# Leaving out the filling multiplications between the first 24 score blocks of an attention kernel

## What is computed

```
q = _fq_sym(q, axis=-1); k = _fq_sym(k, axis=-1); v = _fq_sym(v, axis=2)
attn = jnp.einsum('bhqd,bhkd->bhqk', q, k)
attn = jax.nn.softmax(attn.astype(jnp.float32), axis=-1)
attn = _fq_unsigned(attn, axis=-1)
out = jnp.einsum('bhqk,bhkd->bhqd', attn, v)
```

## Time and profile before

| | |
|---|---|
| three runs | 1157.61, 1159.09, 1159.81 us (median 1159.09) |
| the profiled execution | 1157.37 us |
| span of its instructions | 1155.7 us |
| mean granted TensorE clock | 0.998 |
| preparation up to the first block | 0 to 67.1 us |
| blocks 0 to 23 on TensorE | 67.1 to 80.9 us |
| attention | about 81 to 712 us |

### The profile page before, as it was taken

One profiled execution on the slowest core, in us unless ns is written; L12 is line 12 of the kernel. 1 busy time (PEld: TensorE's weight loads), 2 busy tenths in 40 slices (PEclk: granted clock), 3 DMA queues, 4 the chain that ended last, 5 costly groups with the idle time before them and its releaser, 6 DMA issues.

```text
span 1155.7 us, 24019 instructions
## 1 busy us (share of the span) xinstructions
PE 1042.3 (90%) x8274; PEld 602.8 (52%) x8388; DVE 945.5 (82%) x1732; ACT 892.8 (77%) x1546; POOL 700.7 (61%) x625
## 2 busy tenths in 40 slices
PE   8988888888888888888888888999999999999997
PEld 4744444444444444444444446756654465557775
DVE  6999999999999999999999996963327888943335
ACT  4799999999999999999999997645533576834441
POOL 3027888888787888888788877247751000653432
PEclk9999999999999999999999999999999999999999
DMA  6799998888798788887875775847928002523336
GB/s 195 123 177 139 174 172 161 170 171 172 167 174 169 169 167 175 172 158 164 170 116 110 115 107 92 261 143 213 325 99 329 1 1 52 175 89 106 101 94 235
DMA packets 388799, 176.36 MB, mean 153 GB/s; under 512 B 330413, under 2 KB 373650, under 8 KB 388680
## 3 DMA queue, kind: packets, MB, share of 16 engines
q1 hardware_dynamic: 381976, 157.85, 63.1%
q0 software_dynamic: 6480, 16.77, 4.3%
q10 hardware_dynamic: 224, 0.20, 0.1%
HBM read 52.70 MB, written 43.59 MB: 83 GB/s over the span
## 4 chain that ended last, share of the span: by engine, by line
PE 46%; DVE 27%; ACT 15%; issue 6%; POOL 3%; DMA 2%; SPq 0%; ACTq 0%; POOLq 0%; DVEq 0%
DVE top L425 21%; ACT weight L485 11%; PE bank L234 7%; PE bank L220 7%; PE bank L1206 4%; PE bank L2641 4%; PE bank L1605 3%; PE bank L252 3%; PE bank L2657 3%; PE bank L1193 2%; PE bank L1182 2%; POOL weight L537 1%; PE bank L684 1%; PE bank L1878 1%; PE bank L1623 1%
## 5 line engine op out<-in xcount | busy, mean ns | idle before, releaser
L485 ACT ACTIVATE weight<-bank,bias,sq_all 128x1024 uint8<-128x1024 f32 x512 | 610.1, 1201 | 14.0 <-PE bank L234 8.8
L425 DVE TENSOR_REDUCE top<-bank 128x1 f32<-128x512 f32 (+1 forms) x683 | 610.2, 951 | 11.2 <-PE bank L220 0.9
L537 POOL CAST weight<-turned 128x2048 bf16<-128x2048 uint8 x256 | 479.5, 1895 | 39.0 <-DMA turned<-weight 19.3
L234 PE MATMUL bank<-kT,query 128*128 128x512 bf16 x918 | 284.2, 381 | 26.9 <-ACT weight L485 12.8
L252 PEld LDWEIGHTS bank<-v_sb,weight 128*128 128x128 bf16 x4096 | 172.1, 97 | 104.7 <-POOL weight L537 2.9
L220 PE MATMUL bank<-kT,qspace 64*128 64x512 bf16 x687 | 134.9, 386 | 55.9 <-DVE top L425 55.9
L252 PE MATMUL bank<-v_sb,weight 128*128 128x16 bf16 x4096 | 172.5, 169 | 2.2 <-POOL weight L537 1.8
L220 PE MATMUL bank<-kT,query 128*128 128x512 bf16 x329 | 124.8, 379 | 2.1 <-DVE top L425 1.4
L234 PEld LDWEIGHTS bank<-kT,query 128*128 128x128 bf16 x1024 | 59.7, 96 | 104.2 <-ACT weight L485 62.0
L1848 POOL DMA_INDIRECT dispatched_rows<-qspace,put x32 | 37.2, 1162 | 116.0 <-DVE qspace L2398 106.9
L485 ACT ACTIVATION_READ_ACCUMULATOR weight<-bank,bias,sq_all 128x1 f32 x512 | 101.3, 198 | 0.0
(11 more groups left out here) (351 smaller groups left out, 1459.2 us busy)
## 6 DMA issues: line engine op xcount, KB each, us to landing
dispatched_rows<-zeros SPq DMA_DIRECT2D x32, 524.0 KB, 3.2
answered_rows<-zeros SPq DMA_DIRECT2D x16, 512.0 KB, 3.2
late<-answered_rows SPq DMA_DIRECT2D x16, 512.0 KB, 6.7
erow<-dispatched_rows SPq DMA_DIRECT2D x39, 131.0 KB, 2.1
wgu<-in_L_ffn_w_gate SPq DMA_DIRECT2D x26, 176.0 KB, 3.7
wgu<-in_L_ffn_w_up SPq DMA_DIRECT2D x26, 176.0 KB, 3.6
query<-qspace SPq DMA_DIRECT2D x32, 128.0 KB, 3.2
turned<-weight SPq DMA_TRANSPOSE x256, 3.2
```

The lines of the kernel that those rows point to most:

```text
L234: mm = pe.matmul(unit[u % 2][:, v * 512:(v + 1) * 512], query2[:, t % 2, h, :], kT[:, h // 2, first + v * 512:first + (v + 1) * 512], star ...
L425: ve.tensor_reduce(top[:, first:first + count], bank[:, first % 3:first % 3 + count, :], AX.X, ALU.max).then_inc(s_max, 1)
L485: ac.activation(weight8[:, n % BYTES, u * 1024:(u + 1) * 1024], unit[u], ACT.Exp, bias=bias[:, n:n + 1], scale=sq_all[:, n:n + 1], accum_o ...
L537: po.tensor_copy(weight[:, n % 3, :, :, :].rearrange("p c q two -> p (c q two)"), turned8[:, n % 3, :, :].rearrange("p c q -> p (c q)").bi ...
```

## The change

The two calls of `stir` in the loop over blocks 9 to 23 are left out, on TensorE alone. The waits, blocks and their order stay; so do the passes at the kernel's beginning and the twelve ahead of the first block.

```diff
                     block = fill_maxima(pe, block, 1)
                     while block < LEAD:
-                        stir(2, 4)
                         block = fill_maxima(pe, block, 2)
-                        stir(2, 4)
                         block = fill_maxima(pe, block, 1)
                     copied(("turned values", 3))
```

## The result

The change makes the kernel slower: 1160.87 us against 1158.12 us, medians of 20 runs each, a ratio of 1.0026 (not exactly the quotient of the two medians, 1.0024) with a 95% interval of 1.0014 to 1.0039. That is 2.75 us, a little more than the 0.2%, 2.3 us, that the prediction counted as nothing. One of the 20 runs of the changed kernel took 1172.71 us with a mean clock of 0.949; no trace shows it, and the median doesn't hang on it. The profiled execution took 1161.26 us, with a span of 1159.5 us and a mean granted clock of 0.992 in place of 0.998.

The account below looks back on a forecast made before the run. VectorE's unbroken reductions were taken to bound the loop. Work, gaps, start of the attention and clock each counted 0, so the forecast stayed at the median of before, 1159.1 us, with a range of 1157.6 to 1161.9.

Parts of the forecast that it names:

- the likeliest case: Loop and opening of the attention: TensorE's clock holds, no difference, 1159.1 us; chance 0.47.
- second case: Clock falls in the loop, rises early in the attention: +1.4 us, 1160.5 us; chance 0.38 for 0.2 to 2.8 us.
- The fillings do no work that anyone waits for: Loop, 72.20 to 81.60 us: 4.3 us of TensorE work hidden by VectorE's reductions; removing it gains 0.
- The clock: Loop: TensorE's busy share drops to 44%, yet its clock was taken to hold; cost 0, both ends kept.
- for it: Argument for a clock fall in the loop: 44% is less than any busy stretch in the trace shows.
- What a fall costs: Loop and attention opening: 0.5 us for two cold cycles plus 0.95 us in the opening, together +1.4 us.
- the short fall: Clock low from the loop into the early attention: +1.4 us, ends 0.2 and 2.8 us; chance 0.38.
- a cold cycle: Three blocks of the loop at the low clock: 1.97 us in place of 1.74, 0.23 us more.
- It isn't won back: Attention after a fall: the delay stays, since VectorE and ScalarE each have but 2% free.
- No DMA, no semaphore and no queue is touched: Whole kernel: the change was said to leave transfers, signals and queues alone, so 0 from them.
- four cold cycles and two rises of the clock: Loop and attention opening: upper end of the short fall, 2.8 us, which set the range's top at 1161.9.
- The rival of a long fall: Clock low from 75 to 95 us, up to the first sums of values: +4.1 us, 1163.2 us; chance 0.08.

Follow-up runs that it names:

- e4: Kernel before with all 20 loop fillings thinned to 32 columns in place of 512; +1.47 us against before.
- e6: The change, unchanged, run again beside the kernel before on one chip; median 3.15 us above before.
- e8: The change with nine fillings added in the waits at 733 and 780 us; 1157.90 us, +0.24 us against before (ratio 1.0000).
- e12: The change with 20 multiplications of 32 columns put into TensorE's waits between 8 and 16 us; median 1.63 us above before.
- the clean pair: The change against the kernel before, both with nine fillings at 733 and 780 us; 1157.90 against 1156.73 us.

## Why the prediction was right or wrong

**The number held, the likeliest case didn't.** 1160.87 us lies in the range of 1157.6 to 1161.9, but above the 1159.1 forecast; "slower" by its own measure of 0.2%, which is what came, had a chance of 0.14. What came are the signs of its second case: pairs of 0.61 us, double reductions 1.96 us apart, the first sum of values late. Point by point:

- *The fillings do no work that anyone waits for.* Right. With ten of twenty left VectorE still has no gap.
- *The clock.* This is the step that failed: "Forty-four per cent lies between these two, nearer to the upper row, and no pause comes near to 3 us. I take 0". The row it leaned on was at 62%, and wasn't the sparsest: from 1036.4 to 1039.4 us before was busy for 1.50 of 3.00 us at a clock of 1.00. Neither lasts as long as the loop, and no row showed a clock held at 44%, as the text itself said under "for it", so the trace gave no ground to lean to that side. The run showed a fall after 3.6 us of blocks alone, with no pause over 0.84 us; in the four other profiles with no filling or thin ones in the loop (e4, e6, e8, e12) it came between 74.9 and 76.4 us. The rule of the Trainium skill that was weighed there (TensorE: Matmul & The Clock Gate, A second HAM failure mode: psum-queue depth-cycling) fits this trace better than the forecast did: the clock fell with small pauses only, between groups that cycle through banks, though once in the loop and not again and again.
- *What a fall costs.* Right in sum: +1.4 us was forecast for the short fall, 1.47 us was read at the first sums of values (1.25 to 1.65 us in the other profiles with the same fall) and 1.41 us at the end of the attention; the clean pair gave 1.17 us. The parts: a cold cycle of 1.97 us was forecast and 1.96 measured. More of it lay in the loop than forecast: from the pair at 82.21 against the warm 81.59 three cold cycles make 0.62 us, not two 0.46; the opening then cost 0.85 us. The 0.95 us of the forecast is a slip, for 4.0 / 4.53 x 1.05 is 0.93; the rest of the difference fits a clock that was back at 86.0 us, before the cycle with two units had ended: the two opening cycles lost 0.20 and 0.63 us.
- *It isn't won back.* Right, to a few hundredths, from 97 to 716 us. Both profiles belong to those that lose 0.6 us near 122 us (see the last section), so that doesn't show in their difference.
- *The sum ended there.* "No DMA, no semaphore and no queue is touched" left out the queue that brings TensorE's own instructions. A list that is 40 shorter is fetched at other moments, and one of these packets fell among SyncE's loads at the very end, worth about 1.0 us in one profile and 1.5 us in the other. This term was missing: the short fall's 1.4 us and this 1.0 to 1.5 us make 2.4 to 2.9 us, against the 2.75 us measured. That the result lies in the range is in part luck: the upper end was there for four cold cycles and two rises of the clock, 2.8 us, and what filled it was one fall and a stall that nobody had thought of. The median of three runs that the forecast stood on, 1159.09 us where 20 gave 1158.12, helped by another 1 us.
- *Scatter.* The prediction took the 2.2 us between runs for noise of the measurement. The larger part of the scatter goes with the granted clock, and fillings at two other waits take it out.
- *The rival of a long fall*, up to the first sums of values, didn't happen: the dense opening lifted the clock at 86 us.

## What to carry to other kernels

Multiplications that nobody reads held TensorE's clock here in a stretch that another engine paces, and the stretch to look for is one ahead of dense work, even if its pauses are short. Read the granted clock of all runs and not that of one profile, and price a fall by the records at both levels from the same trace: here the forecast of 1.4 us came out within a quarter of a microsecond. When instructions are removed, ask what the fetching of the list meets at its new times, and test that by padding the list to its old length.

## What was not expected of the hardware

The clock fell in a loop in which TensorE never paused for more than 0.84 us; 20 fillings of 32 columns in the same places didn't hold it, 10 of 512 did. With one packet of the instruction queue among SyncE's issues of loads, the next of them came 0.9 to 1.3 us late, in both profiles in which a packet fell there. And a third thing was seen and not followed: some profiles lose 0.6 us near 122 us, in one of them with TensorE waiting for GpSimd's widening of the weights (line 537), and some don't, with either version of the loop.
